# Late Q and K products in a fused attention and mixture-of-experts kernel: one 128-row matmul or two halves of 64 rows

## The reference

```python
h = _layernorm(x, axis=-1) * (1 + ca) + sa
# attention: the 16x16 matrices Wq, Wk, Wv are shared by the 16 heads
xh = h.reshape(b, t, 16, 16)
q = jnp.einsum('bthc,oc->btho', xh, Wq) * scale
k = jnp.einsum('bthc,oc->btho', xh, Wk) * scale
v = jnp.einsum('bthc,oc->btho', xh, Wv)
scores = jnp.where(j > i, -jnp.inf, jnp.einsum('bihc,bjhc->bhij', q, k))
y = jnp.einsum('bhij,bjhc->bihc', softmax(scores), v).reshape(b, t, d)
x = x + ga * (y @ Wu.T + bu)
h = _layernorm(x, axis=-1) * (1 + cb) + sb
x = x + gb * moe(h)
```

## Time and profile before

| | us |
|---|---|
| timed runs (3), median | 2200.34 |
| lowest and highest of them | 2199.07, 2216.99 |
| profiled execution, span from first to last instruction | 2206.0 |
| PE busy in it | 2061.7 (93%) |
| DVE, ACT, POOL busy | 1693.4 (77%), 1433.2 (65%), 578.3 (26%) |
| first and last X | 107.1, 383.5 |

### The profile page before, as it was taken

The page is one execution under the profiler, slowest core; times in us unless marked ns, Lnnn a source line. Parts: engine busy times, 40 slices in busy tenths (PEclk is TensorE's granted clock), DMA queues, the critical chain, the costliest instruction groups (busy, mean ns, idle before and its releaser), DMA issues. The chain is left out here.

```text
span 2206.0 us, 44494 instructions
## 1 busy us (share of the span) xinstructions
PE 2061.7 (93%) x17787; PEld 1095.9 (50%) x17787; DVE 1693.4 (77%) x2102; ACT 1433.2 (65%) x2797; POOL 578.3 (26%) x827
## 2 busy tenths in 40 slices
PE   7899999999999999999999999999988597999996
PEld 5343333334444444344444433333337486888886
DVE  7688886999999878899999988876628674555553
ACT  5256765778888877678888888888755132344432
POOL 2021110110111111111110100000025563777777
PEclk9699987999999999999999999999979598999999
DMA  6442310111611111441121111000019253555552
GB/s 235 116 83 51 66 37 20 57 57 43 105 58 46 60 41 44 84 75 46 58 70 36 53 49 32 11 1 2 2 55 343 103 183 122 120 117 124 119 124 53
DMA packets 127634, 170.88 MB, mean 77 GB/s; under 512 B 17745, under 2 KB 97106, under 8 KB 126658
## 3 DMA queue, kind: packets, MB, share of 16 engines
q1 hardware_dynamic: 111424, 146.07, 23.8%
q0 software_dynamic: 14016, 17.45, 4.4%
q10 hardware_dynamic: 1986, 4.51, 0.5%
HBM read 91.53 MB, written 77.60 MB: 77 GB/s over the span
## 5 line engine op out<-in xcount | busy, mean ns | idle before, releaser
L848 DVE TENSOR_REDUCE mx<-S 128x2 f32<-128x1024 f32 (+3 forms) x1152 | 1281.7, 1134 | 224.3 <-PE S L744 146.6
L824 ACT ACTIVATE prob<-ST 128x512 f32<-128x512 f32 (+3 forms) x2304 | 1168.6, 559 | 335.8 <-PE ST L765 289.9
L791 PE MATMUL O<-prob,V 128*17 128x256 f32 (+1 forms) x8704 | 678.9, 385 | 0.2 <-POOL prob L713 0.2
L744 PE MATMUL S<-K,Q 48*128 48x512 f32 (+3 forms) x2304 | 562.0, 485 | 25.4 <-DVE mx L848 19.1
L765 PE MATMUL ST<-Q,K 49*128 49x512 f32 (+3 forms) x2304 | 488.4, 420 | 37.3 <-ACT prob L824 31.7
L744 PEld LDWEIGHTS S<-K,Q 48*128 48x128 f32 x2304 | 219.2, 187 | 457.7 <-issue 290.5
L713 POOL TENSOR_SCALAR_AFFINE_SELECT prob<-prob 128x512 f32<-128x512 f32 x128 | 81.2, 635 | 1048.1 <-ACT prob L824 1048.1
L765 PEld LDWEIGHTS ST<-Q,K 49*128 49x128 f32 x2304 | 220.3, 187 | 146.0 <-ACT prob L824 105.1
L791 PEld LDWEIGHTS O<-prob,V 128*17 128x17 f32 x8704 | 145.0, 95 | 281.4 <-issue 272.0
L1622 ACT ACTIVATE sg<-hg 128x512 f32<-128x512 f32 x92 | 55.0, 598 | 160.4 <-PE hu L1550 160.4
L1478 POOL DMA_INDIRECT out<-yo,idt x76 | 122.3, 1609 | 21.4 <-issue 19.0
(11 more groups left out here) (231 smaller groups left out, 1867.8 us busy)
## 6 DMA issues: line engine op xcount, KB each, us to landing
cwb<-cwt SPq DMA_DIRECT2D x76, 256.0 KB, 3.9
lists<-wbd SPq DMA_DIRECT2D x132, 138.0 KB, 2.3
Q<-qs SPq DMA_DIRECT2D x192, 64.0 KB, 2.4
xs<-lists SPq DMA_DIRECT2D x19, 552.0 KB, 3.8
K<-ks SPq DMA_DIRECT2D x18, 512.0 KB, 9.3
wraw<-in_wcat SPq DMA_DIRECT2D x54, 128.0 KB, 2.1
whi_parts<-wcut SPq DMA_DIRECT2D x54, 128.0 KB, 2.1
wlo_parts<-wcut SPq DMA_DIRECT2D x54, 128.0 KB, 2.0
```

The costliest lines, as they stand in the source:

```text
L744: ins = pe.matmul(out[:, ab, 0:w], Q[g, n % QR, p, r * P:(r + 1) * P], K[G % 2][g, p, c * BW:c * BW + w], start=True, stop=not diag)
L791: ins = pe.matmul(O[32 * a:32 * a + VC, c0:c1], V[:, G, k, VC * a:VC * (a + 1)], prob[:, s % NP, a, c0:c1], start=s in FIRST and h == 0, s ...
L824: act.activation(prob[:, s % NP, 2 * p + ab, c0:BW], ST[i % ST_BANKS][:, c0:BW], ACT.Exp).then_inc(s_exp, 1)
L848: dve.tensor_reduce(mx[:, n % 2, a:a + step + 1:step, c], S[slot % S_RING][:, :, 0:w], AX_X, ALU.max).then_inc(s_free, 1)
```

## The change

Each late product is made as two matmuls of 64 rows each: the upper one takes rows 0 to 63 of `wbd` and of the input, the lower one rows 64 to 127. Both write all 128 partitions of a bank of their own, of which 64 hold the product's half. ACT copies 64 partitions of each bank with an instruction of its own. So X takes two turns of the ring in place of one; `fill` counts them so, and the semaphore `wl` gets 8 from each copy. PE's `read` waits, where the turn was an X, for 16 times (product + 1), whichever half it was.

```diff
     def fill(times):
-        i = sum({"ST": 2, "X": 1}.get(kind, 0) for kind, e in events)
+        i = sum({"ST": 2, "X": 2}.get(kind, 0) for kind, e in events)
...
             if kind == "X":
-                turns.append(("X", e))
+                turns += [("X", 2 * e + i) for i in range(2)]
...
                         if kind == "X":
-                            need("wl", s_wl, 16 * (x + 1))
+                            need("wl", s_wl, 16 * (x // 2 + 1))
...
                     elif kind == "X":
-                        i = turn_of["X", e]
+                        i = turn_of["X", 2 * e]
                         b, w, h = LATE[e]
-                        read(need, i - ST_BANKS)
-                        pe.matmul(ST[i % ST_BANKS][:, 0:D], t["wbd"][:, w, :], t["h2"][:, b, 1, h * D:(h + 1) * D],
-                                  start=True, stop=True).then_inc(s_st, 1)
+                        read(need, i + 1 - ST_BANKS)
+                        for ab in range(2):
+                            g = slice(RG * ab, RG * (ab + 1))
+                            pe.matmul(ST[(i + ab) % ST_BANKS][:, 0:D], t["wbd"][g, w, :],
+                                      t["h2"][g, b, 1, h * D:(h + 1) * D], start=True, stop=True).then_inc(s_st, 1)
...
                     elif kind == "X":
-                        i = turn_of["X", e]
-                        need("st", s_st, i + 1)
                         need("wp", s_wp, 3 * e)
-                        act.activation(wraw[:, :], ST[i % ST_BANKS][:, 0:D], ACT.Copy).then_inc(s_wl, 16)
+                        for ab in range(2):
+                            i = turn_of["X", 2 * e + ab]
+                            need("st", s_st, i + 1)
+                            g = slice(RG * ab, RG * (ab + 1))
+                            act.activation(wraw[g, :], ST[i % ST_BANKS][g, 0:D], ACT.Copy).then_inc(s_wl, 8)
```

## The result

| | median us | lowest, highest | runs |
|---|---|---|---|
| kernel before | 2204.32 | 2199.07, 2216.99 | 4 |
| changed kernel | 2265.78 | 2248.61, 2292.65 | 4 |

The ratio is 1.0265, 95% interval 1.0208 to 1.0321: slower by 61 us between the medians, where 19 were forecast. The profiled execution took 2248.61 us with a span of 2246.6.

What follows compares the result with a forecast made beforehand. PE and DVE bound it in turn, DVE between products, with PE making DVE late at each X. 27 x 0.70 + 0.15 = 19.1 us, added to the median 2200.34, gave 2219.4 us; range 2204 to 2238.

Steps and rivals of the forecast that it cites:

- The bound and the place: Between two late products DVE bounds; at each X PE makes DVE late, so PE's delay reaches the end of attention.
- The saving on PE: At each X the halves run together and X ends 0.16 us earlier on PE.
- The added wait: ST behind X now waits for both copies and moves by +0.70 us, 27 times, and +0.15 once.
- 0.66 for both copies: On ACT behind X, the last copy ends 0.66 us after the first starts, 0.28 more than now.
- The clock: A 45 us half-clock stretch cost 16 us; more were called likelier, but left out of the sum as a 0.20 case.
- some 0.6 us: Idle time of PE's ST behind X until ACT's second copy, forecast to occur 27 times.
- The row that I had: In the profile before, the clock fell after S had waited 0.68 us for DVE at 316.19.
- the gain: Rival: ST behind X finds its bank free, only the saving is left, 9.5 us faster, 2190.8 us; chance 0.06.
- the hiding by DVE: Rival: part of PE's delay falls into its waits for DVE, 0 to 14 us, middle 2207; chance 0.15.
- The case with one cold stretch more: Rival: the added wait plus one more half-clock stretch of 16 us, 2235 us; chance 0.20.
- a fourth of 0.59: Part of the main forecast's 0.59 chance counted as lying over 2222.3 us, put at 0.16.

Runs made afterwards that it cites:

- e2: Kernel before, X still one 128-row matmul with one copy, plus one added wait of the ST pair behind X for that copy: 2250.83 us, ratio 1.0223.
- e3: Changed kernel with five bf16 matmuls that nobody reads between X and the ST pair, the wait kept: 2222.29 us, ratio 1.0076 to the kernel before.
- e8: Kernel before with the ST pair behind X waiting for X's single copy, and four unread bf16 matmuls in that wait: 2214.34 us, ratio 1.0000.
- e1: Changed kernel with the ST pair behind X waiting for the first copy alone, not both: 2235.46 us, ratio 1.0111 to the kernel before.
- e5: Changed kernel with the ST pair waiting for the first copy alone and two unread bf16 matmuls in the wait: 2214.10 us, ratio 1.0021.

## Why the prediction was wrong

- *The bound and the place* were right: DVE is starved at each X, runs without a gap between them, and the delay of PE reaches the end in full (offset 23 to 24 us, sum by the rows 22.4).
- *The saving on PE* was right: 0.10 of S to X, the halves together, copies 0.17 earlier (0.16 forecast). It is the gain that the change was worth, and all that it does is to start the copies 0.17 us earlier, since ST waits for them.
- *The added wait* was right in kind and undersized. The term "0.66 for both copies" rested on two exponentials of 128 partitions; the copies of 64 partitions take 0.78. With it 0.70 becomes 0.82, and the sum 22 in place of 19.1.
- *The clock* is the step that failed. "I don't add it to the sum but give it a case", says the prediction, with a chance of 0.20 and one stretch of 16 us: the term was put at nothing, and the runs showed 36 us. The price of a cold microsecond was right: 16/45 = 0.356, and the line through the runs gives 0.353. But it had to be a term of the sum: over 9 runs the changed kernel has 299 us of cold time, 103 more than the kernel before, 103 x 0.353 = 36 us. With the 23 to 24 at equal clock that is the whole difference of the means, 2271.7 - 2211.6 = 60 us; the line makes it add up so, but the 22.4 us worked out from the rows come from elsewhere and agree. The idle time was undersized too, "some 0.6 us" where PE stood still for 0.95. The row that I had, a fall of the clock after one wait of 0.68 us, should have been read against such a wait every ten microseconds. That it is the stall that brings the cold time is shown by e2, e3 and e8; why it comes in one execution and not in the next stays open.
- *The rivals*: the gain and the hiding by DVE are out. The case with one cold stretch more went in the right direction with the wrong number. (A fourth of 0.59 is 0.15, not 0.16, a slip that changes nothing.)

## What to carry to other kernels

When a matmul is split to run side by side, count the turns of the PSUM ring and look who now waits for whose copy: 0.16 us saved on PE cost 0.82 because a copy that ran beside the next matmul moved in front of it. An idle gap on TensorE that comes back, here about every ten microseconds, can have two prices, its length and the clock; here the second was the larger one, 36 of 60 us. Matmuls without a use in such a gap are a cheap test of it, and gave back 44 us in the changed kernel and 36 in the kernel with the wait alone.

## What the runs showed of the hardware that I had not expected

- Two copies of 64 partitions and 256 columns by ScalarE, the first on partitions 0 to 63 and the second on 64 to 127, start 0.40 us apart, more than their full length of 0.378; copies of all 128 partitions overlap (0.17 apart at 128 columns).
- One kernel's runs can lie 2.7% apart with one and the same program: the kernel before from 2186.2 to 2244.8 us over 49 runs, at mean clocks from 0.970 to 0.936. About the line over cold time they scatter by only 3.0 us (standard deviation).
- A stall of 0.55 us of PE behind each X (e1) went with a cold stretch of 188 us in one execution, begun before the first X. With that gap filled (e5) the window from 107 to 430 us had 64 cold microseconds in place of 175, and the changed kernel with its gap filled (e3) had none there, again in one execution each.
